# Two shared 512x512 layers as seven block products each, with smaller weight blocks, in a 16-batch expert kernel

## What is computed

```python
h = silu(noise_encoding(t) @ W1 + b1) @ W2 + b2          # one row for each batch
scale, shift = h @ Wsc + bsc, h @ Wsh + bsh
out = silu(scale * norm(x) + shift) @ W_in + b_in        # norm over both last axes, affine per element
out = silu(scale * norm(out) + shift) @ W_out + b_out
x2 = out + x
# expert e of this batch
g = gelu(x2 @ Wi[e] + bi[e])                             # 512 -> 2048
r = g @ Wo[e] + bo[e] + x2                               # 2048 -> 512
y = layer_norm(r) * gamma[e] + beta[e]
```

## Time and profile before

| what | value |
|---|---|
| median of three runs | 1772.02 us (1771.92 to 1772.20) |
| span of the profiled execution | 1771.7 us |
| what the median holds beside that span | 0.3 us |
| instructions | 22300 |
| granted TensorE clock, mean over the span | 0.999 of full speed (2.4 GHz) |
| HBM read and written | 171.10 MB and 16.81 MB |

### The profile page before, as it was taken

The page is one execution under the profiler, slowest core; times in us unless marked ns, Lnnn a source line. Parts: engine busy times, 40 slices in busy tenths (PEclk is TensorE's granted clock), DMA queues, the critical chain, the costliest instruction groups (busy, mean ns, idle before and its releaser), DMA issues.

```text
span 1771.7 us, 22300 instructions
## 1 busy us (share of the span) xinstructions
PE 1762.8 (99%) x7939; PEld 1454.3 (82%) x7939; DVE 1286.2 (73%) x2147; ACT 977.2 (55%) x1551; POOL 69.0 (4%) x138
## 2 busy tenths in 40 slices
PE   9999999999999999999999999999999999999998
PEld 6888888888888888888888888888888888888887
DVE  6876777767677777767777677677777777777576
ACT  4756554565545656456564555645556555565442
POOL 1100000000000000000000000000000000000000
PEclk9999999999999999999999999999999999999999
DMA  7332232322333233232332313333133232422321
GB/s 292 99 111 75 99 111 85 143 76 99 110 120 111 75 123 110 99 110 72 122 110 99 113 69 122 112 121 110 53 139 113 98 110 75 143 87 75 114 104 68
DMA packets 51666, 189.35 MB, mean 107 GB/s; under 512 B 10467, under 2 KB 14563, under 8 KB 35044
## 3 DMA queue, kind: packets, MB, share of 16 engines
q1 hardware_dynamic: 42770, 183.94, 29.3%
q10 hardware_dynamic: 8786, 3.99, 1.8%
HBM read 171.10 MB, written 16.81 MB: 106 GB/s over the span
## 4 chain that ended last, share of the span: by engine, by line
PE 99%; DMA 1%; SPq 0%; DVE 0%; issue 0%; ACT 0%; POOL 0%; DVEq 0%
PE out_acc L553 39%; PE hid_ps L553 39%; PE blk_ps L553 18%; DMA stage<-in_cond_w 1%; SPq L365 0%; PE out_acc L583 0%; PE out_acc L594 0%; PE out_acc L595 0%; PE out_acc L598 0%; PE hid_ps L571 0%; PE blk_ps L571 0%; PE out_acc L571 0%; PE hid_ps L598 0%; PE hid_ps L594 0%; PE blk_ps L594 0%; PE hid_ps L595 0%
## 5 line engine op out<-in xcount | busy, mean ns | idle before, releaser
L553 PE MATMUL hid_ps<-x_hi,wi_lo 128*128 128x512 f32 x1020 | 396.8, 389 | 0.0
L553 PE MATMUL hid_ps<-x_lo,wi_hi 128*128 128x512 f32 x1020 | 396.8, 389 | 0.0
L553 PE MATMUL hid_ps<-x_hi,wi_hi 128*128 128x512 f32 x1020 | 396.8, 389 | 0.0
L553 PE MATMUL out_acc<-wo_hi,g_hi 128*128 128x512 f32 x1012 | 393.7, 389 | 0.0
L553 PE MATMUL out_acc<-wo_lo,g_hi 128*128 128x512 f32 x1012 | 393.7, 389 | 0.0
L553 PE MATMUL out_acc<-wo_hi,g_lo 128*128 128x512 f32 x1012 | 393.7, 389 | 0.0
L765 ACT ACTIVATE g_sb<-hid_ps,bi_sb 128x512 f32<-128x512 f32 x256 | 175.9, 687 | 311.3 <-PE hid_ps L553 311.0
L893 DVE TENSOR_TENSOR g_lo<-g_sb,g_hi 128x512 fp32r<-128x512 f32 x253 | 173.1, 684 | 190.9 <-ACT g_hi L769 189.2
L723 ACT ACTIVATE wo_hi<-stage 128x512 fp32r<-128x512 f32 x253 | 160.1, 633 | 172.1 <-PE out_acc L553 172.1
L553 PEld LDWEIGHTS hid_ps<-x_hi,wi_lo 128*128 128x128 f32 x1020 | 191.6, 188 | 39.8
L553 PEld LDWEIGHTS hid_ps<-x_hi,wi_hi 128*128 128x128 f32 x1020 | 191.6, 188 | 39.7
(11 more groups left out here) (172 smaller groups left out, 1647.9 us busy)
## 6 DMA issues: line engine op xcount, KB each, us to landing
stage<-in_expert_w SPq DMA_DIRECT2D x128, 1024.0 KB, 4.8
x<-in_xT SPq DMA_DIRECT2D x15, 1024.0 KB, 7.4
out_y<-r_sb SPq DMA_DIRECT2D x15, 1024.0 KB, 5.1
rows<-in_expert_rows SPq DMA_DIRECT2D x16, 512.0 KB, 6.7
mv_all<-mv_dram ACTq DMA_DIRECT2D x30, 128.0 KB, 3.8
affine_sb<-in_affine SPq DMA_DIRECT2D x3, 512.0 KB, 10.0
stage<-in_cond_w SPq DMA_DIRECT2D x3, 512.0 KB, 10.9
x<-in_xT SPq DMA_DIRECT2D x4, 256.0 KB, 4.5
```

What stands on the lines that cost most here:

```text
L553: last = pe.matmul(dst, w[wp], xs[xp], start=start and i == 0, stop=stop and i == 2)
```

## The change

For batches 2 to 15 both shared layers are computed in Strassen's form (one level, with seven products). Activation B and weight A are each cut into four quarters (two chunks of 128 rows by 256 columns); A's four sums are made once, during batches 0 and 1; B's four sums T1 to T4 are made for every batch and layer. Batches 0 and 1 keep the old form.

- **PE.** `seventh` issues 12 matmuls of 256 columns (2 output halves x 2 chunks x 3 terms) in place of a 512-column tile's twelve; seven of them make a layer, two at position 2, two at 3, one at 4, two at 5 (first layer), and the same at 12 to 15 (second layer). They accumulate in two PSUM banks (`BANK_OF`), and sums that two results share are read out in the middle of the accumulation, so products wait for `s_take0` and `s_take1`.
- **Splits.** `h_hi` and `h_lo` become rings of four quarter slots. In tick 1 (10) ACT issues four `rounded`, DVE four `rest` and four `combine`, T1, T3, T2 and T4 in this order with `rest` between them; the other three splits follow in ticks 2 and 3 (12 and 13).
- **Results.** First layer: ACT copies bank 0 out four times (`take_in`), DVE adds bank 1 three times (`take_1_in`); `a_evac` goes, its bias moves into the statistics and into `mean_less`. Second layer: DVE adds four times from bank 0 and three times from bank 1 into x; the bias `b_out` is added to x beforehand by four ACT operations at position 6 (`bout_part`).
- **Order.** `bo_part` moves from position 15 to position 16, that is position 0 of the next batch, ahead of `silu` in ACT's list. The transposes move to positions 5 to 9, the last norm's statistics to 2, `r_centre` to 3, `r_out` to 4. The transposes now wait until y of the batch before is stored.
- **Transfers.** Weight blocks are loaded one at a time (512 KB, ring of three), x and y in four transfers of 256 KB each; a single `mv_all` buffer in place of two; the head's weights get memory of their own.

```diff
-            X_SPLIT: (1,), W_IN: (2, 3, 4, 5),
-            A_TOTALS: (7,), A_CENTRE: (8,), A_AFFINE: (9,), A_SILU: (9,), A_SPLIT: (10,),
-            W_OUT: (11, 12, 13, 14), BO: (15,), X_OUT: (-2,), X_BACK: (-2,), A_BACK: (6,)}
+            X_SPLIT: (1,), W_IN: (),
+            A_TOTALS: (8,), A_CENTRE: (8,), A_AFFINE: (9,), A_SILU: (9,), A_SPLIT: (10,),
+            W_OUT: (), BO: (16,), X_OUT: (-2,), X_BACK: (-2,), A_OUT: (6,), A_BACK: (7,), X_BOUT: (6,)}
...
+A11_B11, A12_B21, S3_T3, S2_T2, S1_T1, A22_T4, S4_B22 = range(PRODUCTS)
+BANK_OF = (0, 1, 1, 0, 0, 1, 0)
+RING_OF = (0, 1, 2, 3, 0, 1, 2)
+PRODUCTS_AT = ({2: (0, 1), 3: (2, 3), 4: (4,), 5: (5, 6)}, {12: (0, 1), 13: (2, 3), 14: (4,), 15: (5, 6)})
+SPLIT_AT = (1, 10)
+TAKE_AT = [(2, 12), (3, 13), (4, 14), (5, 15)]
-R_EVAC, R_STATS, R_CENTRE, R_OUT = 2, 6, 11, 12
-TURN_AT = {2: (0, 1), 3: (1, 6), 4: (6, 11), 5: (11, 16)}
+R_EVAC, R_STATS, R_CENTRE, R_OUT = 2, 2, 3, 4
+TURN_AT = {5: (0, 3), 6: (3, 8), 7: (8, 12), 8: (12, 14), 9: (14, 16)}
...
+            def seventh(b, which, i):
+                before = sevens_before(b, which)
+                weights, slot, bank = weights_of(which, i), RING_OF[i], bank_quarter(BANK_OF[i])
...
+                elif BANK_OF[i]:
+                    pe.wait_ge(s_take1, 3 * before + (1 if i == S3_T3 else 2))
+                else:
+                    pe.wait_ge(s_take0, 4 * before + (1, 2, 3)[(S2_T2, S1_T1, S4_B22).index(i)])
+                pe.wait_ge(s_hlo, splits_of(b, which, i))
+                steps = [(m, c, wp, xp) for m in range(2) for c in range(2) for wp, xp in ((0, 0), (0, 1), (1, 0))]
+                for step, (m, c, wp, xp) in enumerate(steps):
+                    last = pe.matmul(bank[:, m, :], weights[wp][:, c, m * P:(m + 1) * P],
+                                     as_quarter((h_hi, h_lo)[xp][:, slot, :])[:, c, :],
...
+                for b, which in sevens_due(k, SPLIT_AT):
+                    rest(b, which, A11_B11)
+                    combine(b, which, T1)
+                    combine(b, which, T3)
+                    rest(b, which, A12_B21)
+                    rest(b, which, S3_T3)
+                    combine(b, which, T2)
+                    combine(b, which, T4)
+                    rest(b, which, S2_T2)
+                for b, which in sevens_due(k, TAKE_AT[0]):
+                    if which:
+                        take_0_out(b, 0)
+                        rest(b, which, S1_T1)
+                        take_1_out(b, 0)
+                    else:
+                        rest(b, which, S1_T1)
+                        take_1_in(b, 0)
...
-                    for j in range(per):
-                        load_pair(per * b + j, expert)
+                for j in range(HT):
+                    load_block(HT * b + j, expert)
...
+                    if b >= 1 and j == 7:
+                        store_y(b - 1)
```

More of the change, by code:

```diff
@@ L703, in _ @@
                     block_tile(b, 1, m)
+                for b, which, i in products_due(k):
+                    seventh(b, which, i)
                 if 0 <= k < STEPS:
@@ L960, in centre @@
                     dve.wait_ge(s_mean, turn_of(b, which) - 1)
+                less = which and b != 1
+                if less and b:
+                    dve.wait_ge(s_less, b - FIRST_SEVEN + 1)
                 if (b, which) == (0, 0):
@@ L1021, in x2_lo_part, with rest, combine @@
                     .then_inc(s_x2lo, 1)
+            def rest(b, which, i):
+                dve.wait_ge(s_hhi, splits_of(b, which, i))
+                lo_part(as_quarter(h_lo[:, RING_OF[i], :]), source_of(work, i), as_quarter(h_hi[:, RING_OF[i], :])) \
+                    .then_inc(s_hlo, 1)
+            def combine(b, which, t):
+                before = 4 * sevens_before(b, which)
+                b11, b12, b21, b22 = (quarter(work, i, j) for i in range(2) for j in range(2))
+                if t == T1:
+                    dve.wait_ge(s_hlo, splits_of(b, which, A11_B11))
+                    dve.tensor_tensor(b11, b12, b11, ALU.subtract).then_inc(s_comb, 1)
+                elif t == T3:
+                    dve.wait_ge(s_comb, before + T1)
+                    dve.tensor_tensor(b12, b22, b12, ALU.subtract).then_inc(s_comb, 1)
+                elif t == T2:
+                    dve.wait_ge(s_comb, before + T3)
+                    dve.wait_ge(s_hlo, splits_of(b, which, S3_T3))
+                    dve.tensor_tensor(b12, b22, b11, ALU.subtract).then_inc(s_comb, 1)
+                else:
+                    dve.wait_ge(s_comb, before + T2)
+                    dve.wait_ge(s_hlo, splits_of(b, which, A12_B21))
+                    dve.tensor_tensor(b21, b21, b12, ALU.subtract).then_inc(s_comb, 1)
@@ new lines, in take_1_in @@
+            def take_1_in(b, n):
+                before = sevens_before(b, 0)
+                dve.wait_ge(s_product, PRODUCTS * before + (A12_B21, S1_T1, A22_T4)[n] + 1)
+                dve.wait_ge(s_take0, 4 * before + (1, 3, 2)[n])
+                dve.wait_ge(s_hlo, splits_of(b, 0, (S1_T1, S4_B22, A22_T4)[n]))
+                out = quarter(work, *((0, 0), (1, 1), (1, 0))[n])
+                gathered = quarter(work, *((0, 1), (1, 1), (0, 1))[n])
+                dve.tensor_tensor(out, bank_quarter(1), gathered, ALU.add).then_inc(s_take1, 1)
@@ L1238, in _ @@
                         turn(k // HT, q)
+                for b, which in sevens_due(k, TAKE_AT[3]):
+                    if not which:
+                        for m in range(DC):
+                            stats(b, 1, m)
+                for which, n in SUM_HI_AT.get(k, ()):
+                    sum_lo(which, n)
                 if k == SPLIT_REST + 1:
@@ L1316, in _ @@
                         norm_rstd(b, 1)
+                for b, which in sevens_due(k, TAKE_AT[3]):
+                    if not which:
+                        norm_rstd(b, 1)
                 for b in last_norm_due(k, R_STATS):
```

364 lines of the change are left out of this document (288 added, 76 removed).

## The result

| | before | after |
|---|---|---|
| median (range) | 1772.11 us (1771.92 to 1772.26, 4 runs) | 1809.76 us (1809.51 to 1811.67, 4 runs) |
| ratio, 95% interval | | 1.0213 [1.0201, 1.0226] |
| span of the profiled execution | 1771.7 us | 1807.7 us |

The changed kernel is slower by 2.1%, 37.7 us. The page after: span, busy times, the chain that ended last, and the group of instructions before which PE was idle for longest.

The account below looks back on a forecast made before the run. PE bounds the kernel, other engines counting only where PE waits: 1771.7 - 22.4 (columns) + 54.5 (three waits, 13 batches) + 1.7 (batch 2) = 1805.5, with 0.3 around the span 1806 us; range 1757 to 1835.

Parts of the forecast that it names:

- Columns: PE's shared layers: 256-column matmuls at 120 ns make a layer 10.08 us instead of 10.88, saving 22.4 us over 28 layers.
- That rival: Shared products on PE: cheaper matmuls under the same waits, 1784 us by the skill's 109 ns; cheaper matmuls got 0.13.
- the two of costly weight loads: Shared products on PE: weight loads bind at 188 ns, 1943 us, or milder at 133 ns, 1833 us; chance 0.03.
- First wait: Product 0, first layer: `bo_part` delays ACT's chain and DVE's first `rest` by 2.45 us; PE waits 1.9 us.
- Second wait: Product 1, first layer: DVE's `rest` of A12_B21 comes after T1 and T3; PE waits 0.65 us.
- Third wait: Product 2 at position 3, first layer: it reopens bank 1, waiting for `take_1_in` late in DVE's list; 1.6 us.
- 2.45 less: Batch 2's first layer: without `bo_part` there, the waits are 2.45 us less than in later batches, 1.7 us.
- No waits in the second layer: Positions 12 to 15: a tick more, 5.44 us, covers the chain and no `r_evac` is listed, so PE does not idle.
- Engines as sums: Per batch: DVE gets 12 us more, 92 of about 107; ACT 6 us on 61; neither is the limit over sixteen ticks.
- 0.3 us lie around the span: Final sum: 0.3 us added to the profiled span's forecast of 1805.5 us, from the median of 1772.02, giving 1806.
- The last norm only changes places: Last norm and transposes only change places within DVE, without a price; nothing less than a tick shows on PE.

Follow-up runs that it names:

- The move in the old kernel alone: Kernel before the change with only `bo_part` of batches 2 to 15 moved from position 15 to 16: 1798.91 us, ratio 1.0152.
- the opposite test: Fastest kernel (1753.3 us) with `bo_part` put back at position 16 alone: 1779.95 us, ratio 1.0038 to the kernel before.
- the last kernel: Changed kernel with `bo_part` at position 3, products 2 and 3 a tick later, `r_evac` moved, DVE's list reordered and cut in two: 1753.3 us, ratio 0.989.
- the fastest kernel: Against the 1768.7 us kernel, T2, T4 and S2's split and rounding moved behind the next tick's parts, second layer reordered: 1753.3 us, ratio 0.989.

## Why the prediction was right

Forecast 1806 us, measured 1809.76. Point by point, by its own steps:

- **Columns.** 256-column matmuls start 120 ns apart in 1810 of 2240 pairs; the others are mostly the first two of a run (114 and 119 ns) and those right behind a wait. 22.4 us are what 120 ns saves, 0.8 more came from the first two. That each matmul costs 13.3 ns beyond its columns fits both lengths; why it does, no run shows. The Trainium skill (TensorE: Matmul & The Clock Gate, Back-to-back issue gap) has N/2.4 plus 2.5 ns for a warm matmul, an estimated 109 ns for 256 by that page. The trace does not agree: it has 120. That rival falls, as do the two of costly weight loads.
- **First wait.** Forecast 1.9, measured 1.92, at the place and with the releaser named. The move in the old kernel alone and the opposite test show its cause. Two small errors cancel in the number: ahead of product 0, `g_lo` moved by 2.35 us and not by 2.45, and PE started 0.15 us behind the end of the `rest` and not 0.03.
- **Second wait.** 0.65 forecast, 0.55 measured, plus 0.07 behind it. The experiment with `rest` ahead of T1 removed it, so its cause is DVE's order, as argued.
- **Third wait.** 1.6 forecast, 1.53 measured, plus 0.10. It vanished when products 2 and 3 went a tick later. Batch 2: 1.7 forecast, 2.1 measured. The step that was off there is "2.45 less": `affine` was placed by the old kernel's times, and in the new one DVE makes it later, so that `silu` waits for it where no `bo_part` stands ahead (0.35 us in batch 2). Taking `bo_part` away gives back some 2.0 us.
- **No waits in the second layer,** as said. Its spare tick was the reason: without it, 0.46 and 0.17 us appear.
- **Engines as sums.** 92 us of DVE in a batch forecast, 93.0 measured; 67 of ACT, 66.2 measured; PE's share 97% as said.

**What the sum lacked.** The forecast was low by 3.8 us. My step "0.3 us lie around the span" failed: it joined the span of one execution to the median of others. In executions of the kernel before that have both, 1.7 to 2.0 us lie around the span (1773.2 beside 1771.4, for one); after, 1.9 (1809.61 and 1807.7). That is 1.6 us. The same step hid that the span of 1771.7 was itself 1.2 us over the median of 1770.5, which worked the other way. In the span, 3.1 us for slower 512-column matmuls behind each run of 256-column ones had no term, nor had 0.4 for the wait in batch 1; the waits of batches 2 to 15 were 57.0 and not 56.2, and the columns saved 0.8 more than forecast. So the closeness of 1806 to 1809.76 owes something to terms that offset each other, but none of them is over 4 us.

**What the reasons did not reach.** "The last norm only changes places" held for this change, but hid a dependence: `r_evac` was covered by the products ahead of the down product. The prediction had it in DVE's list and never as something that PE waits for, and the miss of the kernel with all products a tick later came from there. Three expectations of shortening DVE's list missed as well, each because I had not followed what stood behind the moved operation: a `rest` moved out of a gap that it had filled, `silu` waited for a later `affine`, and `r_evac`, longer than its gap, pushed T2 back and with it ACT's queue.

What stays open: why the five matmuls behind a 256-column run are slower, and which of the last kernel's several moves removed which of the small waits; no run varied either alone.

## What to carry to other kernels

Price a moved operation at its new place against the slack of the chain that it enters: four ACT operations of 2.5 us cost nothing at one place and 27 us at the next, while the engine had 40% of its time free. Before moving work away from an engine's stream, ask what it covered for the others. In an in-order list an idle spot is filled best with work that waits for nothing there, and what other engines need every tick belongs ahead of what may wait.

## What was unexpected of the hardware

With all first-layer products a tick later, 13 waits of 4.0 to 4.1 us by starts were each followed by a stretch at the 1.2 GHz level (clock 0.50, 427 ns for 512 columns), and one of 2.7 us was not. The clock fell in part 0.3 to 0.6 us before PE resumed, in part 1.2 to 1.4 us behind it. Shorter waits are not safe either: in the kernel after, thirteen waits of 1.92 us left the mean clock of the span at 0.999, and so did those of the old kernel with `BO: (16,)` (1.000); but in the fastest kernel with `BO: (16,)` one of its thirteen waits of 1.91 us, which ended at 707.09, was followed by the same level from 708.54 to 711.96. So the length of a wait alone does not tell whether the clock falls. The first five 512-column matmuls behind 256-column ones start 228 to 236 ns apart, against 227. And a 256-column matmul behind a wait is followed 0.19 to 0.22 us later, not 0.12, by the next.
